# Sizes in place, signed values and all rounded sigmoids through DRAM, in a fused attention and feed-forward kernel

## The reference

```
x = act_qdq(x)                                  # x: layer norm of the residual
up = act_qdq(x @ lpbq_dequant(w_up).T)          # 1536 inner columns
gate = act_qdq(x @ lpbq_dequant(w_gate).T)
sig = fixed_qdq_u16(jax.nn.sigmoid(gate))       # rounded to 1/65536
gate = act_qdq(gate * sig)
o = act_qdq(gate * up)
return o @ lpbq_dequant(w_down).T
```

## Time and profile before

| | |
|---|---|
| median of 3 runs | 1608.95 us |
| profiled execution | 1608.93 us, span 1607.1 us |
| PE busy | 1395.7 us, 87% |
| DVE busy | 1231.8 us, 77% |
| ACT busy | 911.3 us, 57% |
| DMA | 200.56 MB, mean 125 GB/s |
| mean granted TensorE clock | 0.946 of full |

### The profile page before, as it was taken

The page is one execution under the profiler, slowest core; times in us unless marked ns, Lnnn a source line. Parts: engine busy times, 40 slices in busy tenths (PEclk is TensorE's granted clock), DMA queues, the critical chain, the costliest instruction groups (busy, mean ns, idle before and its releaser), DMA issues.

```text
span 1607.1 us, 24370 instructions
## 1 busy us (share of the span) xinstructions
PE 1395.7 (87%) x9268; PEld 788.3 (49%) x9268; DVE 1231.8 (77%) x1934; ACT 911.3 (57%) x1956; POOL 320.9 (20%) x326
## 2 busy tenths in 40 slices
PE   4579999999999999976999999999999203999999
PEld 3356666666666666642444444444444101444444
DVE  7657788888898988746888777688899799745641
ACT  2657787777777778755222222799844696321210
POOL 1124444444444444530111111000000000000000
PEclk9879999999999999978999999999999656999999
DMA  5101111111122221101233332577754995544532
GB/s 203 66 20 63 49 63 63 59 61 62 65 78 80 66 80 54 41 34 53 98 123 116 116 119 98 186 248 248 247 178 170 360 339 185 203 136 160 193 132 79
DMA packets 81812, 200.56 MB, mean 125 GB/s; under 512 B 7712, under 2 KB 7712, under 8 KB 78752
## 3 DMA queue, kind: packets, MB, share of 16 engines
q1 hardware_dynamic: 81696, 199.00, 35.4%
HBM read 128.72 MB, written 70.25 MB: 124 GB/s over the span
## 4 chain that ended last, share of the span: by engine, by line
PE 47%; issue 5%; DVE 1%; DMA 1%; ACT 0%; SPq 0%; POOLq 0%; POOL 0%
PE ffn_banks L1117 30%; PE ffn_banks L1135 16%; DMA ffn_ring<-sigs_dram 1%; PE ffn_banks L1093 1%; DVE ffn_wide L1283 0%; DVE ffn_rises L1288 0%; DVE ffn_peaks L1290 0%; DVE ffn_wide L1282 0%; ACT ffn_rest L1175 0%; ACT ffn_ring L1166 0%; DVE ffn_wide L1421 0%; DVE qg L1383 0%; ACT qg L1175 0%; SPq L1002 0%; PE ffn_banks L1123 0%
## 5 line engine op out<-in xcount | busy, mean ns | idle before, releaser
L1117 PE MATMUL ffn_banks<-ffn_wide,ffn_rest 128*128 128x512 f16 x2304 | 506.2, 381 | 10.4 <-DVE ffn_wide L1283 6.1
L1117 PEld LDWEIGHTS ffn_banks<-ffn_wide,ffn_rest 128*128 128x128 f16 x2304 | 226.1, 98 | 281.1 <-issue 17.3
L1135 PE MATMUL ffn_banks<-ffn_rest,ffn_wide 128*128 128x512 f16 x1152 | 251.2, 382 | 97.0 <-DVE ffn_wide L1428 97.0
L609 ACT ACTIVATE qg<-score_banks,neg_max 128x128 f32<-128x128 f32 (+1 forms) x512 | 207.6, 445 | 53.1 <-DVE neg_max L516 53.1
L1135 PEld LDWEIGHTS ffn_banks<-ffn_rest,ffn_wide 128*128 128x128 f16 x1152 | 113.2, 98 | 235.0 <-issue 100.7
L1175 ACT ACTIVATE ffn_rest<-ffn_banks,ffn_row_back 128x1024 f32<-128x1024 f32 x72 | 79.7, 1107 | 157.1 <-PE ffn_banks L1117 147.4
L1254 ACT ACTIVATE ffn_u_steps<-ffn_ring,ffn_scales 128x1024 int16<-128x1024 f32 x48 | 55.0, 1148 | 158.5 <-DMA ffn_ring<-ups_dram 131.2
L413 POOL TENSOR_TENSOR qg<-qg,per_sum 128x512 f32<-128x512 f32 x64 | 70.1, 1095 | 308.5 <-DVE per_sum L520 308.5
L415 POOL TENSOR_TENSOR qg<-qg,per_sum 128x1024 f32<-128x1024 f32 x64 | 121.1, 1892 | 0.0
L609 ACT ACTIVATION_READ_ACCUMULATOR qg<-score_banks,neg_max 128x1 f32 x512 | 118.9, 232 | 0.0
L657 PE MATMUL ring_banks<-xt,attn_hi 128*128 128x256 f16 x512 | 89.6, 277 | 10.3 <-DVE ct L501 6.3
(11 more groups left out here) (184 smaller groups left out, 2701.6 us busy)
## 6 DMA issues: line engine op xcount, KB each, us to landing
ups_dram<-ffn_rest SPq DMA_DIRECT2D x48, 512.0 KB, 3.1
ffn_ring<-ups_dram SPq DMA_DIRECT2D x48, 512.0 KB, 4.1
ffn_wide<-ups_dram SPq DMA_DIRECT2D x17, 1024.0 KB, 8.0
gates_dram<-ffn_rest SPq DMA_DIRECT2D x24, 512.0 KB, 2.7
ffn_ring<-gates_dram SPq DMA_DIRECT2D x24, 512.0 KB, 4.5
ffn_rest<-w_parts_dram SPq DMA_DIRECT2D x36, 256.0 KB, 4.0
x_in<-in_x SPq DMA_DIRECT2D x16, 512.0 KB, 3.7
qg<-in_ctxt SPq DMA_DIRECT2D x16, 512.0 KB, 4.2
```

Source lines behind the costliest of these rows:

```text
L609: last = act.activation(prob[:, s % 2, h, lo:hi], score_banks[:, h, lo:hi], ACT.Exp, bias=neg_max[:, s % 2, part, h:h + 1], accum_out=row_ ...
L1117: last = pe.matmul(banks[:, pair_of(s), half, :], w[:, m % 2, wp, c, :], xq[:, xp, n, c, :], start=(k == 0), stop=(k == 3 * DC - 1))
L1135: last = pe.matmul(down_banks[:, g % 2, t, :], oq[:, g % 2, op, m, t * P:(t + 1) * P], w_down[:, wp, wk, c], start=(start and k == 0), sto ...
```

## The change

- Every rounded sigmoid, of even chunks too, is stored by `spill` and comes back by `fetch`; ScalarE's second sigmoid and VectorE's second rounding go. `sigs` in DRAM has 48 places, with four semaphores each way. In the first pass `spill(c - 2)` stands behind every chunk from the third on.
- The signed activation of each double is stored in DRAM (`store_signed`), in the slot after its odd chunk, ahead of that slot's fetches. Two slots after its odd chunk ScalarE overwrites the double in `qg` with its size (`sizes`, in place); one double (22) is done behind the up stage, and one (23) is never overwritten and keeps the two reductions. All others need one.
- In the down stage the signed values come back by `load_signed(q, j)`: for the first quarter of the tokens before the stage, for the others during it. `double_order` takes even doubles first, so that these are free early.
- The ring of up doubles has 9 places in place of 8, seven of them in the space of `xq`. The loads for these seven are issued by ScalarE in slots 44 to 47 (`load_early`), as their space comes free. The twelve loads of the down weights move ahead of the last eleven `load_again`.

The declarations of semaphores and of the scratch `signs` (12 x 128 x 4096, int16) are left out here:

```diff
@@ -813,9 +813,9 @@
 ND = NP // 2
-U_RING = 8
-FAR_PLACES = {0: 0, 1: 4, 2: 1, 3: 5, 6: 2, 7: 3}
-NEAR_PLACES = {4: 0, 5: 1}
+U_RING = 9
+FAR_PLACES = {0: 0, 1: 4, 2: 1, 3: 5, 4: 2, 5: 6, 8: 3}
+NEAR_PLACES = {6: 0, 7: 1}
 
@@ -864,9 +864,8 @@
-        far = wide(0, 48, F32, "p (b t) -> p b t", b=6)
+        far = wide(0, 56, F32, "p (b t) -> p b t", b=7)
-        a_size = wide(48, 8, I16, "p (b t) -> p b t", b=2)
@@ -932,14 +933,16 @@
 
-        double_order = [ND - 1] + list(range(ND - 1))
+        double_order = [ND - 1] + list(range(0, ND - 1, 2)) + list(range(1, ND - 1, 2))
+        signs_doubles = io["signs"].rearrange("m p (j c) -> m j p c", c=2 * W2)
+        signs_pairs = io["signs"].rearrange("(q a) p (j c) -> q j p a c", a=2, c=W2)
+        a_pairs = qg[:, :].rearrange("p (q a j c) -> p q j a c", a=2, j=PIECES, c=W2)
         doubles = qg[:, :].rearrange("p (d t) -> p d t", t=2 * W2)
 
-        def both_signs(k):
-            return k % 12 in (1, 3, 6, 8, 11)
-
-        sized = [k for k in range(ND) if not both_signs(k)]
-        signed = [k for k in range(ND) if both_signs(k)]
+        size_slots = [[] for _ in range(NP + 3)]
+        for c, t in [(c, t) for t in range(NP) for c in second[t]]:
+            if c % 2:
+                size_slots[t + 2].append(c // 2)
 
@@ -978,16 +981,15 @@
                 sp.wait_ge(act_peaked, c + 1)
-                sp.dma_start(io["sigs"][c // 2], sig_steps[:, c % 4, :]).then_inc(sig_stored[c % 4 // 2], 16)
+                sp.dma_start(io["sigs"][c], sig_steps[:, c % 4, :]).then_inc(sig_stored[c % 4], 16)
 
             def fetch(c):
-                k = c // 2
-                sp.wait_ge(sig_stored[k % 2], 16 * (k // 2 + 1))
+                sp.wait_ge(sig_stored[c % 4], 16 * (c // 4 + 1))
                 if c < 4:
                     sp.wait_ge(act_peaked, NP - 3 + c)
                 else:
                     sp.wait_ge(a_steps, c - 3)
-                sp.dma_start(chain[:, c % 4, 0:N].bitcast(U16), io["sigs"][k]).then_inc(sig_back[k % 2], 16)
+                sp.dma_start(chain[:, c % 4, 0:N].bitcast(U16), io["sigs"][c]).then_inc(sig_back[c % 4], 16)
 
@@ -995,11 +997,20 @@
                     sp.wait_ge(u_rounded, k - U_RING + 1)
-                elif r in NEAR_PLACES:
+                else:
                     sp.wait_ge(a_steps, NP)
-                else:
-                    sp.wait_ge(filled, 2 * NP - PIECES + 1 + FAR_PLACES[r] % 4)
                 sp.dma_start(u_place(r), up_doubles[d // 2, d % 2]).then_inc(u_in[r], 16)
+
+            def store_signed(d):
+                sp.wait_ge(a_steps, 2 * d + 2)
+                sp.dma_start(signs_doubles[d // 2, d % 2], doubles[:, d, :]).then_inc(a_out[d % 4], 16)
+
+            def load_signed(q, j):
+                last = max(double_order.index(2 * m + j // 2) for m in (2 * q, 2 * q + 1))
+                sp.wait_ge(u_peaked, last + 1)
+                for d in (4 * q + j // 2, 4 * q + 2 + j // 2):
+                    sp.wait_ge(a_out[d % 4], 16 * (d // 4 + 1))
+                sp.dma_start(a_pairs[:, q, j], signs_pairs[q, j]).then_inc(a_back[q][j % 2], 16)
 
@@ -1025,37 +1036,43 @@
                         load_gate(c)
-                    if c % 2 and c >= 3:
+                    if c >= 2:
                         spill(c - 2)
-                if t >= NP - 2:
-                    for k in range(2):
-                        load_again(1 + 2 * (t - NP + 2) + k)
+                for d in size_slots[t + 1]:
+                    store_signed(d)
                 for c in second[t]:
                     if c == 0:
+                        spill(NP - 2)
                         spill(NP - 1)
-                        fetch(1)
-                        fetch(3)
-                    if c % 2 and c >= 5:
+                        for b in range(4):
+                            fetch(b)
+                    if c >= 4:
                         fetch(c)
                 store_piece(s)
-            for k in range(5, ND):
+            for slot in size_slots[NP + 1:]:
+                for d in slot:
+                    store_signed(d)
+            for k in [7, 8] + list(range(10, 13)):
                 load_again(k)
+            for b in range(2):
+                sp.wait_ge(parts_stored[b], 16 * IC)
+            for b in range(3):
+                last = [k for k in range(len(stage_uses)) if k % 3 == b][-1]
+                sp.wait_ge(stored[b], 16 * (last // 3 + 1))
+            sp.wait_ge(u_rounded, 1)
             for m in range(IC):
-                if m == 0:
-                    sp.wait_ge(a_steps, NP)
-                    for b in range(2):
-                        sp.wait_ge(parts_stored[b], 16 * IC)
-                    for b in range(3):
-                        last = [k for k in range(len(stage_uses)) if k % 3 == b][-1]
-                        sp.wait_ge(stored[b], 16 * (last // 3 + 1))
                 k, r = divmod(m, DC)
                 unit = r * (IC // DC) + k
                 sp.dma_start(w_down_units[:, unit], io["w_parts"][2 * IC + unit]).then_inc(w_down_in[k], 16)
+            for k in range(13, ND):
+                load_again(k)
+            for q in range(PAIRS):
+                load_signed(q, 0)
 
             def load_u(g, q):
                 r = g * PAIRS + q
                 if r < 4:
-                    sp.wait_ge(u_rounded, ND - 2 + r // 2)
+                    sp.wait_ge(u_rounded, 17 + r // 2)
                 else:
@@ -1075,6 +1092,8 @@
                         load_u(g, q)
+                    if g < 2 * (PIECES - 1) and g % 2 == 0:
+                        load_signed(q, g // 2 + 1)
                     if g >= 2 and q == 0:
@@ -1191,9 +1210,22 @@
 
+            def sizes(d):
+                act.wait_ge(a_out[d % 4], 16 * (d // 4 + 1))
+                act.activation(doubles[:, d, :], doubles[:, d, :], ACT.Abs).then_inc(a_sized, 1)
+
+            def load_early(k):
+                r, d = (k - 1) % U_RING, double_order[k]
+                for c in (2 * d, 2 * d + 1):
+                    was_stored(act, NP + c)
+                act.dma_start(u_place(r), up_doubles[d // 2, d % 2]).then_inc(u_in[r], 16)
+
             act.wait_ge(u_backed, 1)
             for t in range(NP):
                 evacuate(NP + t)
+                for k in range(1, U_RING + 1):
+                    if k - 1 in FAR_PLACES and t == NP - PIECES + FAR_PLACES[k - 1] % 4:
+                        load_early(k)
                 for c in first[t]:
@@ -1212,25 +1244,10 @@
                                    scale=sc["g_step"]).then_inc(sig_ready, 1)
-                for c in second[t]:
-                    if c % 2:
-                        continue
-                    if c < 4:
-                        act.wait_ge(act_peaked, NP - 3 + c)
-                    else:
-                        act.wait_ge(sig2_used, c // 2 - 1)
-                    act.activation(chain[:, c % 4, :], steps_of_piece[:, c, :], ACT.Sigmoid,
-                                   scale=sc["g_step"]).then_inc(sig2_ready, 1)
-
-            def sizes(n):
-                if n >= 2:
-                    act.wait_ge(u_peaked, sized[n - 2] + 1)
-                act.activation(a_size[:, n % 2, :], doubles[:, double_order[sized[n]], :], ACT.Abs).then_inc(a_sized, 1)
-
-            act.wait_ge(a_steps, NP)
-            act.wait_ge(filled, 2 * NP)
-            sizes(0)
-            sizes(1)
+                for d in size_slots[t]:
+                    sizes(d)
+
+            late = [d for slot in size_slots[NP:] for d in slot if d != ND - 1]
             act.wait_ge(u_scaled, 1)
@@ -1241,9 +1258,9 @@
                     act.wait_ge(u_peaked, k - 2)
-                if k in sized[2:]:
-                    sizes(sized.index(k))
                 act.activation(u_of(k), src, ACT.Abs, scale=sc["u_per"]).then_inc(u_rounded, 1)
+                if 0 <= k - 4 < len(late):
+                    sizes(late[k - 4])
 
@@ -1359,8 +1376,8 @@
                         dve.wait_ge(parts_stored[c], 16 * IC)
-                    if c % 2 and c >= 5:
-                        dve.wait_ge(sig_stored[c % 4 // 2], 16 * ((c - 4) // 4 + 1))
+                    if c >= 4:
+                        dve.wait_ge(sig_stored[c % 4], 16 * (c // 4))
                     dve.wait_ge(sig_ready, c + 1)
@@ -1372,14 +1389,8 @@
                 for c in second[t]:
-                    if c % 2:
-                        dve.wait_ge(sig_back[c // 2 % 2], 16 * (c // 4 + 1))
-                        sig = chain[:, c % 4, 0:N].bitcast(U16)
-                    else:
-                        sig = sig_steps[:, c % 4, :]
-                        dve.wait_ge(sig2_ready, c // 2 + 1)
-                        dve.tensor_scalar(sig, chain[:, c % 4, :], SIG, SIG - 1.0, ALU.mult, ALU.min).then_inc(sig2_used, 1)
-                        dve.wait_ge(sig2_used, c // 2 + 1)
+                    dve.wait_ge(sig_back[c % 4], 16 * (c // 4 + 1))
+                    sig = chain[:, c % 4, 0:N].bitcast(U16)
```

(33 more changed lines are left out.)

## The result

The changed kernel takes 1642.72 us (median of 4 runs), the kernel before 1608.42 us beside it: a ratio of 1.0221, 95% interval 1.020 to 1.0242. It is 34.3 us slower. The direction was forecast, and 1642.7 lies within the range of 1598 to 1646; the size was not: 13.6 us were forecast.

What follows compares the result with a forecast made beforehand. Time was taken as T, plus the gap, plus a TensorE-bound, unchanged down projection. T moves 24.6 + 4 + 8 = 36.6 us, the gap shrinks by 23.0: 13.6 us slower, 1622.5 us, range 1598 to 1646.

Steps and rivals of the forecast that it cites:

- The gap: From the second pass's end to the first down-projection matmul: 64.4 us in place of 87.4, saving 23.0 us.
- the tail: In the gap, the up-value load standing last in the DMA queue: 1 us added (0 to 8).
- the signs named: VectorE waits of 3.0 to 3.7 us, last product near 1302, 25 reductions, TensorE gap some 95 us, down part 251 us.
- T: End of the second pass over the activation: 1265.3 us before, forecast to move by 36.6 us to 1301.9.
- First pass: Gate loads wait behind sigmoid stores in SyncE's queue and hold up ScalarE: 4 us on T (0 to 9).
- Rounds: Second-pass fetches stand behind SyncE's wait for the last odd chunk; five slots take 33.0 us, T 24.6 us later.
- L: One round in the second pass, from a VectorE product's end to the next one's start: 4.2 us (3.7 to 5.6).
- Early loads: Seven loads issued by ScalarE in slots 44 to 47 share the DMA engines with fetches: 8 us (3 to 17).
- Prefetch holds: Rival: SyncE's wait in the second pass costs nothing, the full saving of 23 to 26 us stays, 1584; chance 0.13.
- A saturated DMA: Rival, joined with long rounds: a slot's 1.85 MB needs 357 GB/s, above the 339 seen; 1640; joint chance 0.22.
- long rounds: Rival, second pass: landings of 5.1 us, five slots 40 us, time 1660, half of that 1640; joint chance 0.22.
- my own forecast: Main case: L from 3.9 to 4.8 with middle values of the other terms, time 1608 to 1638; chance 0.50.

Runs made afterwards that it cites:

- number 9: Number 5 with each first load of signed values directly ahead of the up values it meets, not six signed loads first: 1592.0 us, 0.9899 of the kernel before.
- number 5: Number 1 with even chunks' sigmoids taken and rounded again as in the kernel before, so only signed values newly go through DRAM: 1595.3 us.
- number 1: The changed kernel with each second-pass slot's fetches ahead of its store of signed values: 1611.2 us.
- number 2: The changed kernel with the wait for the last odd chunk kept ahead of the fetches, but the signed store issued behind them: 1633.6 us.
- number 6: The kernel before with all 48 rounded sigmoids stored and fetched, and no signed values in DRAM: 1607.2 us.
- number 3: The changed kernel with a slot's gate loads ahead of its sigmoid stores in the first pass: 1644.0 us.
- number 7: The changed kernel with a slot's sigmoid stores behind its store of the up piece in the first pass: 1639.8 us.
- number 4: The changed kernel without loads from ScalarE; SyncE loads the seven up doubles behind the second pass: 1645.8 us.
- number 8: The changed kernel with all stores of rounded sigmoids issued by GpSimd in place of SyncE: 1639.5 us.

## Why the prediction was right or wrong

**The bound, the gap, and the mechanism were right.** The gap shrank from 87.4 to 66.7 us (64.4 forecast); the missing 2.3 us are the tail, sized at 1 us and really 3.2, the wait for the first up values that number 9 removes from the gap of number 5:

```profile
DVE ffn_wide L1426 <- ACT ffn_u_steps L1271: 3.4, 2, 3.2
```

(The parts given for the transfers in the gap add up to 23.1 MB, not 23.5; that is 1 us, and VectorE sets the gap either way.) The down projection took 250.4 us. Of the signs named, the waits (67.4 us in 21, 3.2 each) and the 25 reductions came; the last product stood at 1322 and not near 1302, and TensorE's gap was 113.8 us and not 95. The rounds are in the chain as described, and numbers 1, 2 and 6 show that the wait, not the bytes and not the fetches, makes them. That the range held the time, near its upper end, is owed to its width and not to the sum, which was 20.7 us short.

**The shift of T was mis-sized: 36.6 us forecast, 56.8 measured.** Three terms of the sum are short, all the same way; against the forecast they are 6.8 + 7.7 + 5.8 = 20.3 us.

- *First pass: 4 us in the sum, 10.8 measured* (first product 1174.7, not 1163.9; 11.2 between the means of equal passes). The step that failed is a plain one. The hand count had given 2 to 3 us for each seven slots, and the pass has 28 slots: by itself that is 8 to 12 us. I took 4 with a range to 9, as if slack would absorb the rest; ScalarE's 12 free us didn't. My reason, a gate load behind a store in SyncE's list, was half right at best: moving the gate load ahead in its slot did nothing beyond the scatter (number 3), moving the stores behind the up piece gave back some 4 us (number 7), and 3 to 4 us have no cause yet.
- *Rounds: 126.0 us from first product to last, 133.7 measured without early loads* (number 4). Five slots took 34.9 to 35.0 us, not 33.0: read from the chain, L is 4.5 and not 4.2, and the ten products between the rounds take 12.5 us and not 12.0. The twelve landings between 1191 and 1270 in the chain average 4.0 us; I had taken 3.7, the median of fetches in an uncrowded queue plus the store's transfer, although held 4.9 and 5.1 too.
- *Early loads: 8 us in the sum, 13.8 measured,* near the bound of 17. I had taken half, on the argument that ScalarE's issues fall late in a round; in fact three landings in a row grew to between 7.4 and 8.65 us, and the next to 5.8. The three and the fourth exceed the average of 4.0 by 13.9 us together. That DMAs from different issuers share the same 16 engines, as the Trainium skill has it (DMA: Bandwidth & Descriptors, "Issuing engines are not separate DMA queues"), points this way, and the trace agrees: loads from ScalarE's queue cost SyncE's fetches 13.8 of the 17.3 us that they occupy.

**The rivals.** *Prefetch holds* is refuted by 67.4 us of waits. *A saturated DMA* is false for the changed kernel (0.80 busy in the second pass) and true one step later, when the wait is gone (number 1, 1.01 busy). Its figure of 339 GB/s was low: number 1 ran at 376. The gap moved 394 GB/s, number 5's 407. The share of some 358 GB/s in the Trainium skill (HBM Reference, "Specifications (TRN2)") didn't bind this core, as that page says for a core alone.

**The chances** put 0.72 on slower, rightly, and 0.22 on long rounds near 1640, where it fell, for another reason than named there: L, at 4.5, stayed inside the band of my own forecast, and it was not one large term but three small ones, all the same way.

## What to carry to other kernels

An engine that issues DMAs in the order of its list turns each wait into a wait for everything behind it (here 22 us by the wait alone): before a store is put into such a list, read what stands behind it, and put what an engine will ask for next in front. Two edits may cost 34 us together when one adds a wait and the other adds work behind it, though each, well placed, costs nothing, so time them apart; here one half was worth 1% and the other nothing. And when a hand count gives a drift per period, multiply it by the number of periods before setting slack against it.

## What the runs showed of the hardware

- Stores, fetches and loads mixed ran at 376 GB/s with all 16 DMA engines busy (number 1), and mostly loads at 394 to 407 in the gap. The 339 GB/s of the earlier trace rows, at a share of 1.00 in a window of 4 us, was no ceiling.
- A share near 1 is therefore no measure of what still fits; number 5 moved 305 GB/s at 0.86, a rate per share of 355, and number 1 reached 376.
- GpSimd took 0.54 to 0.87 us to issue one 256 KB store (number 8), beside 0.32 for SyncE, and in the first pass these landed in 4.1 us in the median, against 2.2 from SyncE in the changed kernel.
- A 256 KB fetch issued 3.1 us or more behind the last 512 KB store or weight load landed in 2.7 to 2.8 us, one issued up to 2.4 us behind it in 4.3 to 5.2 (number 2).
